# Attention scores in 12-bit halves on half-array tiles, and half of the projections moved into the attention steps

## The reference, cut to what matters

```
x = x + attention(_layernorm(x), W_dq, W_uq, W_dkv, W_uk, W_uv, W_o)
x = x + ffn(_layernorm(x), ...)
x = x + deltanet(_layernorm(x), ...)
x = x + ffn(_layernorm(x), ...)
```

```
k_eff = (W_dq.T @ W_uq.T @ W_uk).reshape(nh, hs, n_kvl)
v_eff = transpose((W_uv.T @ W_o.T).reshape(n_kvl, nh, hs), (1, 0, 2))
c_kv  = x @ W_dkv.T
q     = x @ W_dq.T @ W_uq.T
attn  = einsum('bhql,bkl->bhqk', einsum('bqhd,hdl->bhql', q, k_eff), c_kv) / sqrt(hs)
attn  = softmax(where(causal, attn, -inf))
y     = einsum('bhql,hld->bqhd', einsum('bhqk,bkl->bhql', attn, c_kv), v_eff)
```

## Time and profile before

| | |
|---|---|
| median of 3 runs | 1483.3 us (1480.09 to 1485.56) |
| profiled execution: time, span | 1484.99 us, 1482.8 us |
| busy in the span: PE, DVE, ACT, POOL | 1224.4, 986.0, 591.5, 345.6 us |
| PE weight loads | 770.9 us |
| instructions | 32889 |
| DMA | 61.69 MB, 77795 packets |

### The profile page before, as it was taken

How to read it: one execution, slowest core, us unless ns; L and a number is a source line. 1 busy time by engine, 2 the same in 40 slices (tenths; PEclk the granted TensorE clock), 3 DMA queues, 4 the chain that set the end, 5 groups by cost and what they waited for, 6 DMA issues and landing times. The chain is left out here.

```text
span 1482.8 us, 32889 instructions
## 1 busy us (share of the span) xinstructions
PE 1224.4 (83%) x13850; PEld 770.9 (52%) x13850; DVE 986.0 (66%) x2188; ACT 591.5 (40%) x999; POOL 345.6 (23%) x495
## 2 busy tenths in 40 slices
PE   5638899999999999998999726558798868689993
PEld 3314444444444444436888613335565656578883
DVE  4527788888888888835754656676868372375546
ACT  3415565556565656575322222112232212142222
POOL 2313200000000000001211256535563312221114
PEclk9869999999999999998999958878898988889996
DMA  5692333344433334200000000001111101000003
GB/s 177 115 155 95 137 44 44 45 57 59 59 45 44 45 45 61 28 2 1 1 1 1 1 29 10 22 21 37 31 33 26 37 20 18 2 0 1 0 1 113
DMA packets 77795, 61.69 MB, mean 42 GB/s; under 512 B 41168, under 2 KB 63824, under 8 KB 77520
## 3 DMA queue, kind: packets, MB, share of 16 engines
q1 hardware_dynamic: 76496, 57.18, 21.9%
q10 hardware_dynamic: 1152, 2.41, 0.5%
HBM read 38.20 MB, written 20.97 MB: 40 GB/s over the span
## 5 line engine op out<-in xcount | busy, mean ns | idle before, releaser
L651 DVE TENSOR_REDUCE maxima<-psum 128x1 f32<-128x512 f32 (+3 forms) x768 | 395.2, 553 | 65.5 <-PE psum L426 47.6
L619 ACT ACTIVATE weights<-psum 128x1024 f32<-128x1024 f32 (+3 forms) x384 | 296.2, 813 | 198.5 <-PE psum L454 142.0
L423 PE MATMUL psum<-k_stack,q_stack 96*128 96x512 bf16 (+3 forms) x768 | 236.1, 329 | 33.1 <-DVE maxima L651 33.0
L451 PE MATMUL psum<-q_stack,k_stack 99*128 99x512 bf16 (+3 forms) x768 | 202.2, 326 | 1.2 <-ACT weights L619 1.2
L423 PEld LDWEIGHTS psum<-k_stack,q_stack 96*128 96x128 bf16 x768 | 74.6, 97 | 196.2 <-DVE maxima L651 121.9
L468 PE MATMUL psum<-weights,v_rows 128*17 128x512 f32 (+3 forms) x1536 | 161.1, 491 | 0.0
L392 POOL TENSOR_TENSOR residual<-residual,att_o 128x256 f32<-128x256 f32 x32 | 23.2, 724 | 486.6 <-DVE att_o L686 486.6
L848 PE MATMUL psum<-f_xT,f_weights_hi 128*128 128x512 f32 x384 | 123.9, 404 | 0.0
L913 ACT ACTIVATE f_gates<-psum,ffn_biases 128x512 f32<-128x512 f32 x72 | 49.5, 687 | 155.9 <-PE psum L854 155.9
L426 PE MATMUL psum<-mask_scores,identity 128*128 128x128 bf16 x512 | 110.6, 221 | 0.0
L1284 PE MATMUL psum<-d_w_qkb,d_hT 128*128 128x260 f32 x128 | 48.4, 514 | 66.2 <-DVE d_attnT_k_kb_v L1454 55.6
(11 more groups left out here) (160 smaller groups left out, 2253.1 us busy)
## 6 DMA issues: line engine op xcount, KB each, us to landing
qk_parts<-a_parts SPq DMA_DIRECT2D x32, 384.0 KB, 2.6
q_stack<-qk_parts SPq DMA_DIRECT2D x96, 128.0 KB, 7.4
k_stack<-qk_parts SPq DMA_DIRECT2D x96, 128.0 KB, 8.1
residual<-in_x SPq DMA_DIRECT2D x8, 512.0 KB, 7.6
out_x<-residual SPq DMA_DIRECT2D x8, 512.0 KB, 3.8
ffn_weights<-in_ffn_w ACTq DMA_DIRECT2D x1, 2048.0 KB, 8.8
systems<-d_a_rows SPq DMA_DIRECT2D x32, 64.0 KB, 1.8
d_systems<-systems SPq DMA_DIRECT2D x4, 512.0 KB, 3.3
```

The costliest lines, as they stand in the source:

```text
L423: m = e.matmul(bank[bk][:, 0:width], self.qst[st][0:SCORE_ROWS, h, qb * P:(qb + 1) * P], self.kst[st][0:SCORE_ROWS, h, k0:k0 + width], sta ...
L451: m = e.matmul(out[:, 0:width], self.kst[st][0:SCORE_ROWS + MAX_ROWS, h, kb * P:(kb + 1) * P], self.qst[st][0:SCORE_ROWS + MAX_ROWS, h, q0 ...
L619: e.activation(self.weights[n % 2][:, 2 * pair:2 * pair + 2, 0:width], self.st_pair[pair][:, :, 0:width], ACT.Exp, scale=HS ** -0.5).then_ ...
L651: e.tensor_reduce(self.maxima[n][:, h, qb, k0 // BANK:k0 // BANK + 1], next_max_bank()[:, 0:width], AXIS_X, ALU.max, negate=True).then_inc ...
```

## The change

**Parts.** q and k are split into two parts of type float32r, which keeps some 12 bits: ACT rounds, DVE subtracts. ACT's second rounding and POOL's subtraction go. The DRAM tensor holds two float32 parts (512 KB a store).

**Rows.** Three products (`SPLIT`) fill 48 rows. Of a unit's four heads two lie in rows 0 to 63 (`HALF`) and two in rows 64 to 127; the stacks are [128, 2, 1024]. Two rows more carry the maxima in two parts. Matmuls of the two halves alternate and write different banks. Still 12 loads a unit, each of 16 rows x 2 heads x 1024 float32, 128 KB.

**Maxima.** `pairs` has 20 items a unit. An item takes two banks, one per half of the rows; where the width is at most 256, a bank holds two heads side by side, under one mask matmul and one reduce. The mask now comes first and runs on all 128 rows.

**Order.** `order()` writes one list for all engines. Its prologue projects groups 0 and 1, then groups 2 and 3 between the first 26 maxima items. Groups 4 to 7 are projected in the steps, their ten items (two turns, two latents, four of q/k, two of v) one a step, from steps 4, 20, 52 and 68 on. Banks are handed out by the same list: seven in the prologue, 4, 5 and 6 (`RING`) in the steps, for everything that is not a score or a value. The stacks of the first three units are loaded in two halves of columns, after group 0's and after group 1's stores. Some weights used only at the start share memory with an exponential buffer.

**Norm.** The subtract and multiply of every layer norm moves from DVE to POOL, with a negated mean.

```diff
@@ Norm.gpsimd (Norm.vector loses the same loop) @@
+        e.tensor_scalar(k.negmean[:, g], k.moments[:, g, 0], -1.0, None, ALU.mult).then_inc(*s["negmean"].did(i))
...
+        for j, t in enumerate(tiles):
+            for w in unmet(s["rstd"](i), s["negmean"](i), s["turned"](i - len(self.slots), KT - 1) if i >= len(self.slots) else None):
+                e.wait_ge(*w)
+            e.tensor_scalar(self.slot(i)[:, j, :], k.xr[:, t, :], k.negmean[:, t:t + 1], k.rstd[:, t:t + 1], ALU.add, ALU.mult
+                            ).then_inc(*s["normed"].did(i, j))
@@ Attention @@
+    SPLIT = ((0, 0, 1), (0, 1, 0))
+    ROWS = 3 * HS
+    HALF = P // 2
+    LEAD = 6
+    PROLOGUE_BANKS, RING = (0, 1, 2, 3, 4, 5, 6), (4, 5, 6)
...
-            self.qst = [sb(f"q_stack{i}", [P, HPU, T], BF16) for i in range(STACKS)]
+            self.qst = [sb(f"q_stack{i}", [P, 2, T], F32R) for i in range(STACKS)]
...
+        self.pairs = []
+        for qb in range(QB):
+            for c in range(((qb + 1) * P + BANK - 1) // BANK):
+                width = min(BANK, (qb + 1) * P - c * BANK)
+                self.pairs += [(qb, c, width, heads) for heads in ([(0, 1)] if width <= BANK // 2 else [(0,), (1,)])]
...
+    def order(self):
+        per = len(self.pairs)
...
+            late[min((u + 1) * per + 2, len(maxima)) - 1] = ("negmax", u)
+        def project(g):
+            return ([("turn", g, kt) for kt in range(KT)] + [("lat", g, n) for n in range(2)] +
+                    [("qk", g, *p) for p in self.PROJECTED] + [("v", g, j) for j in range(0, TPG, 2)])
...
+        self.taken, lead = 0, per + self.LEAD
+        more = project(2) + [("norm", 4)] + project(3)
+        self.prologue = [("norm", 0), ("norm", 1), ("const", 0), ("const", 1), ("const", 2)] + project(0) + [("norm", 2)]
+        self.prologue += project(1) + [("norm", 3)]
+        for i in range(lead):
+            self.prologue += take(i + 1) + more[i * len(more) // lead:(i + 1) * len(more) // lead]
+        self.during = [[] for _ in range(len(self.steps) + 3)]
+        for g in range(4, GROUPS):
+            first = (g // 2 - 2) * UNITS_PER_B * len(self.unit_steps) + 4 + g % 2 * 16
+            for i, item in enumerate(project(g)):
+                self.during[first + i].append(item)
+            if g > 4:
+                self.during[first - 4].append(("norm", g))
+        for n, (u, kb, qc) in enumerate(self.steps):
+            self.during[n] += take(lead + -(-per * (n + 1) // len(self.unit_steps)))
+            if kb == (qc + 1) * TPG - 1:
+                self.during[n + 2].append(("out", u, qc))
@@ sync: load(u, halves) @@
+            for n in range(len(self.SPLIT[0])):
+                for which, dst in ((0, self.qst[st]), (1, self.kst[st])):
...
+                    for j in range(2):
+                        for w in unmet(self.stack_free(u), s["k_ones"](st), *sent):
                             e.wait_ge(*w)
+                        r = j * self.HALF + n * HS
+                        e.dma_start(dst[r:r + HS, :, cols].bitcast(F32), src[j]).then_inc(...)
@@ tensor: make(item), of kind "max" @@
+                for j in range(2):
+                    if diagonal:
+                        e.matmul(out[j][:, 0:len(heads) * width].rearrange("p (a x) -> p a x", a=len(heads))[:, :, width - P:width],
+                                 k.ident16[:, :], k.mask16[:, :].rearrange("p (o x) -> p o x", o=1).to_broadcast([P, len(heads), P]),
+                                 start=True, stop=False, skip_group_check=True)
+                for i, h in enumerate(heads):
+                    for j in range(2):
+                        rows = slice(j * self.HALF, j * self.HALF + self.ROWS)
+                        m = e.matmul(out[j][:, i * width:(i + 1) * width], self.qst[st][rows, h, qb * P:(qb + 1) * P],
+                                     self.kst[st][rows, h, k0:k0 + width], start=not diagonal, stop=True, skip_group_check=True)
@@ tensor: scores(n, pair) @@
             for j in range(2):
+                rows = slice(j * self.HALF, j * self.HALF + self.ROWS + 2)
+                m = e.matmul(bank[2 * pair + j][:, 0:width], self.kst[st][rows, pair, kb * P:(kb + 1) * P],
+                             self.qst[st][rows, pair, q0:q0 + width], start=True, stop=not self.diagonal(n))
+            for j in range(2 if self.diagonal(n) else 0):
+                m = e.matmul(bank[2 * pair + j][:, 0:P], k.mask16[:, :], k.ident16[:, :], start=False, stop=True)
@@ tensor: the steps (scalar: exps(n, 0), copies of the items, exps(n, 1), turn_out(n - 1)) @@
+        for n, items in enumerate(self.during):
+            half = len(items) // 2
+            if n < len(self.steps):
+                scores(n, 0)
+            for item in items[:half]:
+                make(item)
+            if n < len(self.steps):
+                scores(n, 1)
+            for item in items[half:]:
+                make(item)
+            if 0 < n <= len(self.steps):
+                values(n - 1)
@@ vector, ahead of everything but the constants @@
+        for st in range(STACKS):
+            for j in range(2):
+                e.memset(self.kst[st][j * self.HALF + 32:(j + 1) * self.HALF, :, :].bitcast(F32), 1.0).then_inc(*s["k_ones"].did(st))
```

More of the change, by code:

```diff
@@ L353, in sync @@
         k.load_x_sync(e, range(2, GROUPS))
[L354 to L355 removed]
+        for item in self.prologue:
+            send(item)
+            if item == ("qk", 0, *self.PROJECTED[-1]):
                 for u in range(STACKS):
[L357 to L365 removed]
@@ L437, in turn, with stacked @@
[L437 to L447 removed]
+        def stacked(u, half):
+            n = len(self.SPLIT[0]) - 1
+            return s[f"stack_in{u % STACKS}"](u, half if u < STACKS else 1, n, 1, 1)
@@ L448, in scores @@
+        def scores(n, pair):
+            u, kb, qc = self.steps[n]
+            st = u % STACKS
+            q0, width = self.span(n)
+            for w in unmet(stacked(u, qc), s[f"max_in{st}"](u, 1, 1), s["k_ones"](st),
+                           *([s["exp"](n - 1, pair)] if n else [self.prologue_end.get(b) for b in range(4)])):
                 e.wait_ge(*w)
             for j in range(2):
-                h, out = 2 * pair + j, bank[2 * pair + j]
-                m = e.matmul(out[:, 0:width], self.kst[st][0:SCORE_ROWS + MAX_ROWS, h, kb * P:(kb + 1) * P],
-                             self.qst[st][0:SCORE_ROWS + MAX_ROWS, h, q0:q0 + width], start=True, stop=not diagonal)
@@ L470, in values @@
             m.then_inc(*s["values"].did(n))
-            return (u, qc) if last else None
-        def output(u, qc):
-            bk = next_max_bank()
-            for w in unmet(s["oT_out"](u, qc), free[bk]):
-                e.wait_ge(*w)
-            for j in range(TPG):
-                m = e.transpose(bank[bk][:, j * P:(j + 1) * P], self.oT[(2 * u + qc) % 2][:, j * P:(j + 1) * P], k.ident[:, :])
-            m.then_inc(*s["oT_turned"].did(u, qc))
-            free[bk] = s["att_o"](u, qc)
@@ L532, in tensor @@
-        while max_at < self.lead:
-            max_tile()
-        waiting, finishing = None, None
-        for n, (u, kb, qc) in enumerate(self.steps):
-            scores(u, n, kb, qc, 0)
-            max_tile()
-            scores(u, n, kb, qc, 1)
-            max_tile()
-            if finishing:
-                output(*finishing)
-            max_tile()
-            finishing = values(waiting) if waiting is not None else None
-            waiting = n
-            max_tile()
-        if finishing:
-            output(*finishing)
@@ L548, in tensor @@
-        output(*values(waiting))
+        for item in self.prologue:
+            make(item)
+        for n, items in enumerate(self.during):
+            half = len(items) // 2
[6 more added lines that the diff above has]
+            for item in items[half:]:
+                make(item)
+            if 0 < n <= len(self.steps):
+                values(n - 1)
@@ L611, in turn_out @@
                 e.activation(self.oT[c % 2][:, :], bank[7][:, :], ACT.Copy).then_inc(*s["oT_out"].did(u, qc))
-        for n, (u, kb, qc) in enumerate(self.steps):
-            width = (qc + 1) * BANK - max(qc * BANK, kb * P)
-            for pair in range(2):
-                w_free = s["values"](n - 2) if n >= 2 else s["v_mm"](GROUPS - 1, TPG - 2)
-                for w in unmet(s["scores"](n, pair), w_free):
-                    e.wait_ge(*w)
-                e.activation(self.weights[n % 2][:, 2 * pair:2 * pair + 2, 0:width], self.st_pair[pair][:, :, 0:width],
-                             ACT.Exp, scale=HS ** -0.5).then_inc(*s["exp"].did(n, pair))
-            if n:
+        for item in self.prologue:
+            copy_out(item)
@@ L736 @@
+        for st in range(STACKS):
+            for j in range(2):
+                e.memset(self.kst[st][j * self.HALF + 32:(j + 1) * self.HALF, :, :].bitcast(F32), 1.0).then_inc(*s["k_ones"].did(st))
+        e.memset(bank[7][:, :], 0.0).then_inc(*s["o_zero"].did())
+        for item in self.prologue:
```

(4 more changed lines are left out.)

608 lines of the change are left out of this document (276 added, 332 removed).

## The result

The changed kernel takes 1640.5 us (median of four runs, 1625.6 to 1731.9) against 1484.4 for the kernel before in the same comparison: a ratio of 1.102, 95% interval 1.094 to 1.111. The prediction was 1459 us. The change makes the kernel ten per cent slower, which is also above the upper end of the range.

What follows compares the result with a forecast made beforehand. PE was taken to bound attention's steps, with DVE close, and DMA the prologue. From 1485.0: prologue -54, unit length -4, projections +40, tail -4, FFN -4, sum -26, so 1459 us; own range 1435 to 1490, whole range 1390 to 1530.

Steps and rivals of the forecast that it cites:

- Prologue: Start of attention, before the first scores: 170 us becomes about 116, taken as -54; bounds 105 to 130.
- FFN: Both FFNs' start: normalization on POOL lets DVE deliver first biases some 2 us sooner; -4 us for two.
- Steps, PE: PE's time a unit in attention's steps: half-row pairs save 7.3 us, changes between full array and strips add 4.2.
- the sum of 27.5: PE's time a unit in the steps: 30.6 before, less its stalls, - 7.3 + 4.2 = 27.5 us.
- rival C: Steps: the row halves do not run beside each other; unit 38 us, total 1547; chance 0.11, shared with exposed weight loads.
- Steps, DVE: Unit length in the steps, with reduces and bank waits: 32.0 us for 32.27, -4 in all; bounds 28.5 and 38.
- stall like today's: Steps: PE's waits for DVE's reduces stay at 0.45 us a step, leaving a unit at 30 to 35 us.
- B's sign: Steps: units without projections at 35 us or more, with PE's waits for reduces above 0.5 us a step.
- rival B: Steps: the three-bank ring serializes; unit 35.2 us, projections 56, total 1522, slower; chance 0.27.
- the walk's 30: Steps: the larger of PE and DVE in each step, added up step by step, gives about 30 us a unit.
- Projections in the steps: Groups 4 to 7, one item a step over 40 steps: +40 us, about PE's own time; lowest 20, highest 60.
- Tail: Last 16 steps of attention: with scores halved ACT bounds; -4 us.

Runs made afterwards that it cites:

- projections_first: The changed kernel with all eight groups projected in the prologue, ahead of the steps: 1581.1 us.
- the spread loads alone: The kernel before, with only the stack loads of units 0, 1 and 2 issued after groups 2, 5 and 6: 1459.5 us, ratio 0.981.
- full_rows: The changed kernel with every score and maxima matmul reading all 128 rows (filled q stack, smaller exponent scale; not attention's output): 1576.7 us.
- same_half: The changed kernel with both heads' score and maxima matmuls reading rows 0 to 63 (not attention's output): 2061.1 us.
- half_masks: The changed kernel with each causal mask added by matmuls over 64 rows in each half, same output: 1540.2 us.
- filler: The changed kernel with one more bf16 matmul of 512 columns on all rows ahead of each step's first scores: 1662.1 us.
- short reduces: The changed kernel with maxima reduces reading a quarter of their columns, exponent scaled down (not attention's values): 1530.3 us.
- half_masks_short_reduces: The changed kernel with masks over 64 rows and maxima reduces reading a quarter of their columns (not attention's values): 1472.8 us.

## Why the prediction was wrong

**Prologue, right in the sum, in part by luck.** The first scores were forecast near 116 us and came at 115.04; -54 was -55. One DMA-only gap of 12.9 us stood before 84 us, as allowed for. But it ended at 79.1 and not at 84, and from there to the first scores it took 36 us and not 32: two errors of about 4 us cancel. The -55 has two parts: with all eight groups projected first (projections_first) the first scores still come 21 us sooner than in the kernel before, as much as the spread loads alone gave there (21.7), and the other 34 are projections put off into the steps.

**FFN, a small term.** -4 was -0.6. The first biases do come 4.9 us sooner after the last output (5.4 us for 10.3), but the first FFN matmul only 0.8 sooner (12.0 for 12.8), because PE then waits for POOL's normalization. The same code behind attention takes 799.6 to 807.4 us in the other runs, so a term of 4 us can't be told from these.

**The largest term that failed was not written down: every duration of the steps was taken at full clock.** Of the 184 us between 1459 and the profiled 1643, the clock is about 80, the unit's length 76 (+72 for -4), the projections 13 to 15 and the tail 12. Before, the granted clock was 1.00 there with matmuls on 96 and 99 of 128 rows at 97% busy. The change puts 48 and 50 rows in their place, and the prediction carried 0.235 us over from FFN matmuls that read all rows. Measured, TensorE runs some 209 of 697 us at 1.2 GHz, which costs about 80 us of the 214 (78 by one reckoning, 80 by the other). Reading all rows took it away (1.00 throughout), as work on all rows did in the regular steps, and as fewer waits did; reading only one half at a time made it worse. The number of rows is shown as a cause: full_rows and same_half both run a pair's heads one after the other and differ in the rows, and with them in the changes of tiling. The type is float32r in both, so the type alone isn't the cause. It is not the only one: at the same 48 and 50 rows, with both halves in use, the mean clock of attention is 0.79 to 0.99, by the order, the waits, the masks and the place of the projections. What starts and ends one low stretch is not settled: half_masks has fewer matmuls on all rows than the changed kernel and about the same idle time in a unit, and 65 us at the low level for 215. The runs that read other rows also change the numbers in the array, which no run tested by itself; filler, projections_first and half_masks, whose output is attention's, move the clock without that.

**"Steps, PE": the sum of 27.5 was mis-sized.** At full clock PE is busy 86.56 of 100 us, 32.4 a unit of 37.4. The pair's steady cost, 0.24 for the forecast 0.235, and the concurrency were right (rival C as told falls: same_half takes 0.23 more a pair). What failed is the cover: few pairs stand behind another pair. In the unit that ends at 569.06, 33 of the 48 pairs stand behind something other than a pair. About 0.1 us shows at each of them even without a change of tiling (half_masks), 3.3 us of the excess of 4.9. Another 0.6 is in the sum's base: 30.6 for PE before, where the earlier trace rows give 457.20 / 473 x 32.27 = 31.2 busy. The rest, about 1 us, is not assigned. half_masks, with its masks on half rows, still has PE busy 28.4 a unit (84.36 of 100 us). The share of the loads is worked out, no run took them away. The Trainium skill's rule on weight loads and row groups (TensorE: Matmul & The Clock Gate, Part 3) had been made part of C with 8.4 us; the trace bears out about 40% of that, a pair behind another pair on the same two halves showing none of it (0.24 us). So that the measured 37.4 lies next to C's 38 is a coincidence of the sum. The changes of tiling were priced at 4.2 us for 42, 0.1 each, and taking 56 of them away with half-row masks gave 3.8, 0.07 each: that term was about right.

**"Steps, DVE": 30 to 35, "I take 32.0", was too low.** Over PE's sum it left 32.0 - 27.5 = 4.5 us of waiting a unit, and 5.0 were measured: nearly right in size, while the PE sum under it was 4.9 higher. But it was no "stall like today's": in the list of waits from which the 0.45 us a step came, the changed kernel has 0.63, above the 0.5 that the prediction had named as B's sign, and PE's idle time is 5.0 us a unit where it was 1.1. So rival B's mechanism is there (short reduces take 3.0 us off); its 35.2 was exceeded, 37.4, because B too was built on the low PE sum. With both causes gone a unit takes 30.9, near the walk's 30.

**Projections in the steps.** +40, PE's own time, was 55 in full_rows and 62 in half_masks_short_reduces. Rival B's chain gave 56, and that is nearer. Ahead of the steps the same four groups cost 149.1 - 115.0 = 34 us (35 with half-row masks, 156.2 - 120.8), so moving them into steps that are already full loses some 21 to 27 us even at full clock. In the changed kernel the clock comes on top: projections_first has about 40 us less of it.

**Tail, wrong in sign.** 16 steps were to gain 4, because ACT would bound them with scores halved. In the last unit PE is busy 20.87 of 24 us, ACT 15.94: PE bounds it still. full_rows takes 8 us more than the kernel before for the last two units (58.2 for 50.3), at full clock; half_masks_short_reduces takes 50.2.

The bill from first scores to last output: unit length 14.1 x (37.4 - 32.27) = +72, the last two units +8, projections +53 to +55, low clock +78 to +80, in sum 211 to 215 for 214. (In the kernel before, too, the first unit's output came 1.3 us after its share of 13 steps; the 53 leaves that out.) The projections and the last two units are full_rows' figures, so with the 80 from full_rows the sum must close; the 78 comes from the changed kernel's own clock.

## What to carry to other kernels

Before halving the rows of matmuls that fill most of PE's time, price the granted clock: a kernel that holds 1.00 with 96 rows may not with 48 (here 0.54 to 0.99 in the mean of the attention, by what stands around those matmuls). A packed pair is only as cheap as in a row of pairs; between matmuls of another shape it costs up to 0.2 us more (0.43 for 0.24), of which the change of tiling is shown and a part of the weight load is inferred, so bring masks and other small matmuls to the same tiling as the work around them. And when a change has a good part and a bad one, run the good part alone: here the loads' place was worth 1.9%, while the projections put off into the steps gave 34 us in the prologue and cost 55 or more behind it.

## What the runs showed that was not expected

- PE at 100% busy, mostly with matmuls on 48 and 50 of 128 rows, was granted 0.50 for the whole of 300 to 350 us (same_half), while half_masks_short_reduces, which reads both halves side by side, has 0.99 in the mean of the attention.
- Adding 512 columns of full-row work to each step lengthens a unit by 3.2 us (12 x 0.22 = 2.6 are its columns) and keeps the clock at 1.00 from 500 to 800; leaving the masks out lowered it from 1.00 to 0.90 from 500 to 600.
- Shortening DVE's reduces, which leaves every matmul as it was, took PE's time at the low level from 215 to 51 us.
- The same two heads on full rows, one after the other, cost only 1.3 us a unit more than beside each other on half rows (38.8 against 37.4): what the pair saves is largely lost again in changes of tiling, exposed loads and waits.
